# One layer on eight cores: transposes a step later, one-hot products on VectorE, and a later norm

## The reference, cut to what matters

```python
xn = layernorm(x)
q, k, v = split_heads(xn @ w_qkv.T + b_qkv)          # 16 heads of 64
q = silu(q);  k = softmax(k, over the tokens)
out = q @ (k.T @ v)                                  # linear attention, kv is 64 x 64 per head
out = layernorm(out, ln_g, ln_b)
gate = sigmoid((xn @ w_g1.T + b_g1) @ w_g2.T + b_g2) # 1024 -> 64 -> 1024
attn = (out * gate) @ w_out.T + b_out
# mixture of experts: 8 experts, top 2 per token, 769 slots per expert for 2048 tokens
top_vals, top_idx = top_k(xn @ Wr.T, 2);  w = softmax(top_vals)
pos = position of each (token, choice) in its expert # cumsum of the one-hot choices
expert_in[expert, pos] = xn[token]                   # dropped where pos >= capacity
ffn[token] = sum_k w[token, k] * (expert_in @ We)[expert_k, pos_k]
y = x + attn + ffn
```

## Time and profile before

| what | before |
|---|---|
| median of 3 runs | 545.15 us (543.25 to 560.69) |
| the profiled execution: its own time | 543.36 us |
| its span (slowest core, core 1) | 541.8 us |
| spans of the 8 cores | 532.8 to 541.8 us |
| mean granted TensorE clock, core 1 | 0.969 |
| PE busy | 463.1 us (85%) |
| DVE / ACT / POOL busy | 289.1 (53%) / 225.0 (42%) / 203.5 us (38%) |

### The profile page before, as it was taken

How to read it: one execution, slowest core, us unless ns; L and a number is a source line. 1 busy time by engine, 2 the same in 40 slices (tenths; PEclk the granted TensorE clock), 3 DMA queues, 4 the chain that set the end, 5 groups by cost and what they waited for, 6 DMA issues and landing times.

```text
span 541.8 us, 9152 instructions; the slowest of 8 cores (532.8 to 541.8 us)
## 1 busy us (share of the span) xinstructions
PE 463.1 (85%) x3072; PEld 237.3 (44%) x3072; DVE 289.1 (53%) x621; ACT 225.0 (42%) x353; POOL 203.5 (38%) x169
## 2 busy tenths in 40 slices
PE   0778999989979897997977877899999879986996
PEld 0345655544545443543424433444544434432442
DVE  5666552057776661646654664422122424639996
ACT  3497765365455531564535644433433424200000
POOL 2254346000000139331023363345446633349753
PEclk9999999999999999999988999899999979996998
DMA  8898976999407999899898269377379997356995
GB/s 204 262 290 261 203 189 132 140 169 165 78 2 256 344 164 149 97 118 146 97 134 152 67 138 295 85 200 247 117 217 253 232 313 260 141 183 233 318 315 219
DMA packets 38131, 102.73 MB, mean 190 GB/s; under 512 B 4544, under 2 KB 4672, under 8 KB 37888
## 3 DMA queue, kind: packets, MB, share of 16 engines
q0 software_dynamic: 15520, 44.34, 45.0%
q1 hardware_dynamic: 18880, 47.21, 28.2%
q10 hardware_dynamic: 3680, 10.52, 5.4%
HBM read 93.97 MB, written 37.75 MB: 243 GB/s over the span
## 4 chain that ended last, share of the span: by engine, by line
PE 65%; issue 9%; DVE 8%; DMA 6%; ACT 5%; POOL 2%; SPq 2%; DVEq 1%; another core or an unknown queue 0%; ACTq 0%; PEldq 0%; POOLq 0%
PE PS L315 58%; PE PS L319 7%; DMA wlate<-x_tm 3%; ACT stage L323 2%; SPq L79 2%; POOL stage L696 2%; DMA wlate<-wv_t 1%; DVE bst L891 1%; DMA vq<-eo_d 1%; DVE nm L754 1%; ACT vq L323 1%; DMA eo_d<-vq,dtab 1%; ACT stage L330 1%; DVE stage L339 1%; POOL wr L334 1%
## 5 line engine op out<-in xcount | busy, mean ns | idle before, releaser
L315 PE MATMUL PS<-wr,xnt 128*128 128x512 bf16 x512 | 119.6, 391 | 13.7 <-DVE wr L334 7.0
L315 PE MATMUL PS<-xnt,wr 128*128 128x512 bf16 x512 | 119.6, 380 | 0.5 <-ACT vq L323 0.5
L315 PEld LDWEIGHTS PS<-wr,xnt 128*128 128x128 bf16 x512 | 49.8, 100 | 76.0 <-issue 23.1
L315 PE MATMUL PS<-wlate,stage 128*128 128x512 bf16 x288 | 70.9, 398 | 5.0 <-issue 4.8
L315 PEld LDWEIGHTS PS<-xnt,wr 128*128 128x128 bf16 x512 | 47.8, 98 | 51.5 <-issue 3.5
L330 ACT COPY stage<-PS 128x1024 bf16<-128x1024 bf16 x56 | 56.4, 1008 | 16.4 <-PE PS L319 16.2
L334 POOL TENSOR_TENSOR stage<-stage 128x1024 bf16<-128x1024 f32 x16 | 34.2, 2138 | 45.5 <-DVE stage L331 39.8
L315 PE MATMUL PS<-wr,stage 128*128 128x512 bf16 x224 | 50.6, 379 | 0.2 <-issue 0.2
L338 DVE TENSOR_SCALAR vq<-PS,wslot_f 128x512 bf16<-128x512 f32 x24 | 18.0, 750 | 58.6 <-PE PS L315 45.6
L315 PEld LDWEIGHTS PS<-wlate,stage 128*128 128x128 bf16 x288 | 28.0, 101 | 35.9 <-issue 10.2
L994 POOL DMA_INDIRECT eo_d<-vq,dtab x24 | 25.0, 1041 | 48.3 <-ACT vq L323 32.7
(11 more groups left out here) (153 smaller groups left out, 645.4 us busy)
## 6 DMA issues: line engine op xcount, KB each, us to landing
wlate<-x_tm SPq DMA_DIRECT2D x20, 512.0 KB, 6.2
eo_d<-stage SPq DMA_DIRECT2D x4, 2048.0 KB, 15.3
vq<-eo_d SPq DMA_DIRECT2D x16, 512.0 KB, 5.9
xn_d<-stage SPq DMA_DIRECT2D x16, 256.0 KB, 6.6
wlate<-we POOLq DMA_DIRECT2D x2, 2048.0 KB, 34.2
wr<-we POOLq DMA_DIRECT2D x2, 2048.0 KB, 31.1
wb_d<-we POOLq DMA_DIRECT2D x8, 512.0 KB, 18.9
wlate<-wb_d SPq DMA_DIRECT2D x8, 512.0 KB
```

Source lines behind the costliest of these rows:

```text
L315: return PE.run(lambda e: e.matmul(out, l, r, start=start, stop=stop), *toks, sig=sig)
```

## The change

Five edits:

1. **K**: the transposes run three steps behind the projection and K times V four steps behind, with a fourth `eT` buffer. The loop has one more step.
2. The first two Q projections are issued in the steps at the end of the K loop; their Silus stay where they were.
3. The five one-hot products move from POOL to DVE, each a route piece of its own. At b = 0 the units 0 to 4 take the four spreads and the first product; at b = 1 unit 0 takes two products, units 1 and 2 one each. `r_table` stays at b = 1, u = 4.
4. `g_hidden` takes its bank in turn with the Q projections (banks 0 and 1), not bank 6.
5. `a_norm` is cut in two: `a_shift` (the small DVE step) stays at odd u; the activation is queued at the next even u, behind that unit's Tanh. `m_trans(0)` uses bank 1.

```diff
-        eT = [ek[:, 512 * i:512 * (i + 1)] for i in range(3)]
+        eT = [ek[:, 512 * i:512 * (i + 1)] for i in (0, 1, 2, 5)]
...
-            SPREAD = 5
+            SPREAD = 4 + NV
...
-            def r_hot():
-                for v in range(NV):
-                    tk["hot"] = GP.run(lambda e, v=v: e.tensor_tensor(
-                        hot_v[:, :, v, :], hot_c, wide(vals[:, v, :], NJE), ALU.mult),
-                        tk["hc"], tk["vals"])
-            piece(r_hot)
+            def r_hot(v):
+                def f():
+                    tk["hot"] = tt(DV, hot_v[:, :, v, :], hot_c, wide(vals[:, v, :], NJE),
+                                   ALU.mult, tk["hc"], tk["vals"])
+                return f
+            for v in range(NV):
+                piece(r_hot(v))
...
-                ex_tok[j] = act(eT[j % 3][:], bank[bk], AF.Exp, nb_tok[j], kv_tr.get(j - 3),
+                ex_tok[j] = act(eT[j % 4][:], bank[bk], AF.Exp, nb_tok[j], kv_tr.get(j - 4),
...
+            q_turn = itertools.cycle((0, 1))
+            def q_mm(b, oc):
+                bk = q_at[b, oc] = q_bank()          # next(q_turn)
+                for c in range(HC):
+                    p = mm(bank[bk], wv3[2][:, c, 128 * oc:128 * (oc + 1)],
+                           xnT[:, c, 512 * b:512 * (b + 1)], c == 0, c == HC - 1,
+                           t_wq, btok[bk], sig=(c == HC - 1))
+                return p
-            for j in range(NJ + 3):
-                if 2 <= j < NJ + 2:
-                    k_trans(j - 2)
+            for j in range(NJ + 4):
+                if 3 <= j < NJ + 3:
+                    k_trans(j - 3)
                 if j < NJ:
                     k_proj(j)
-                if j >= 3:
-                    k_kv(j - 3)
+                if NJ < j < NJ + 3:
+                    q_ahead[j - NJ - 1] = q_mm(0, j - NJ - 1)
+                if j >= 4:
+                    k_kv(j - 4)
                 if j < NJ:
                     k_exp(j)
...
             def q_proj(b, oc):
-                bk = oc % 2
...
+                p = q_ahead[oc] if b == 0 and oc in q_ahead else q_mm(b, oc)
+                bk = q_at[b, oc]
...
             def g_hidden(b):
-                bk = 6
+                bk = q_bank()
...
+            def a_shift(t):
+                s = t % 2
+                nm_tok[t] = ts(DV, nmr[:, s:s + 1], mv[:, s, 0:1], rs[:, s:s + 1], ALU.mult,
+                               -1.0, ALU.mult, ag2[t], n_tok.get(t - 2))
             def a_norm(t):
                 s = t % 2
-                n = ts(DV, nmr[:, s:s + 1], mv[:, s, 0:1], rs[:, s:s + 1], ALU.mult,
-                       -1.0, ALU.mult, ag2[t])
                 k = 1 + a_pair(t)
-                n_tok[t] = act(n_sb[t % 8], PS[:, 1024 * k:1024 * (k + 1)], AF.Identity, n,
+                n_tok[t] = act(n_sb[t % 8], PS[:, 1024 * k:1024 * (k + 1)], AF.Identity, nm_tok[t],
...
-                xtr[J], xgt_tok[J] = m_turn(0 if J <= BESIDE else J % 2, AC, ...
+                xtr[J], xgt_tok[J] = m_turn(1 if J == 0 else 0 if J <= BESIDE else J % 2, AC, ...
...
-                    if route and u < SPREAD:
+                    for _ in range({(1, 0): 2, (1, 1): 1, (1, 2): 1}.get((b, u), b == 0 and u < 5)):
                         route.pop(0)()
...
+                    t = 4 * (b - 1) + u // 2
                     if z >= 0:
                         a_gate(z // 8, z % 8)
+                    if u % 2 == 0 and 0 < t <= NT:
+                        a_norm(t - 1)
+                    if z >= 0:
                         a_z(z // 8, z % 8)
                     if b >= NB:
                         m_beside(b - NB, u)
-                    if 1 <= b <= NB:
+                    if 0 <= t < NT:
                         if u % 2 == 0:
-                            a_out(4 * (b - 1) + u // 2)
+                            a_out(t)
                         else:
-                            a_norm(4 * (b - 1) + u // 2)
+                            a_shift(t)
```

More of the change, by code:

```diff
@@ L1 @@
 import contextlib
+import itertools
 import numpy as np
@@ L767, in k_trans @@
                 for i in range(4):
-                    p = tr(bankh[bk][:, 128 * i:128 * (i + 1)], eT[j % 3][:, 128 * i:128 * (i + 1)],
+                    p = tr(bankh[bk][:, 128 * i:128 * (i + 1)], eT[j % 4][:, 128 * i:128 * (i + 1)],
                            ex_tok[j], btok[bk], sig=(i == 3))
@@ L822, in k_final, with q_bank @@
                 k_sum.extend([least, weights, most, last])
-            for j in range(NJ + 3):
-                if 2 <= j < NJ + 2:
-                    k_trans(j - 2)
+            q_ahead = {}
+            q_at = {}
+            q_turn = itertools.cycle((0, 1))
+            def q_bank():
+                return next(q_turn)
+            def q_mm(b, oc):
[8 more added lines that the diff above has]
+                    k_trans(j - 3)
                 if j < NJ:
                     k_proj(j)
-                if j >= 3:
-                    k_kv(j - 3)
+                if NJ < j < NJ + 3:
+                    q_ahead[j - NJ - 1] = q_mm(0, j - NJ - 1)
+                if j >= 4:
+                    k_kv(j - 4)
                 if j < NJ:
@@ L853, in build_nc @@
             n_tok = {}
+            nm_tok = {}
             ntr = {}
@@ L988, in m_trans @@
             def m_trans(J):
-                xtr[J], xgt_tok[J] = m_turn(0 if J <= BESIDE else J % 2, AC, xg[xg_at(J)], xgT[J % 3], xg_tok[J],
+                xtr[J], xgt_tok[J] = m_turn(1 if J == 0 else 0 if J <= BESIDE else J % 2, AC, xg[xg_at(J)], xgT[J % 3], xg_tok[J],
                                             mo_pe.get(J - 3))
```

## The result

The changed kernel takes 525.75 us (median, 521.93 to 528.42), the kernel before, on the same chip, 547.31: a ratio of 0.965, interval 0.958 to 0.971. It is faster, inside the range 513 to 532, 4.75 us above the forecast of 521. Some executions of every kernel run a few per cent slower on the cores of one die (cores 0 to 3 or 4 to 7) or of both; the medians include them, the ratios don't. The profiled execution took 527.23 us; its slowest core is now core 3, where before it was core 1.

A forecast was written before the change was run, and what follows sets the result against it. PE was taken to set the time, with its waits for other engines' queues to be won. 6.0 + 1.9 + 15.1 + 2.5 - 1.5 = 24.0 us off 543.36 gave 519.4, as a median 521 us, range 513 to 532.

The forecast's parts named there:

- K, -6.0: K loop: transposes three behind remove all but 0.3 of PE's 6.3 us of waits for the exponential.
- tail and table, -1.9: K's end to slot table: one 3.7 us PE hole before the third Q projection (+0.8), included in the table's 1.9 gain.
- Products: One-hot products before the slot table: 2.0 us each on DVE against 3184 ns on POOL, so the table starts earlier.
- Norm and gate, -15.1: Blocks 2 to 4: of 15.8 us of PE waits, all but 0.35 and 0.3 go.
- clock, -2.5: PE's half-speed stretches after waits: 2.5 of 3.3 us come back, bounds 0 and 5.
- the circle: Attention blocks: norm, tanh, product and statistics wait on each other, 6.51 us norm to norm against 5.19 of PE work.
- DMA, +1.5: Gather of J = 3 lands behind expert weights on POOL's queue, so PE waits 1.5 us, bounds 0 and 6.2.
- the DMA rival: Gathers for J = 3 land no earlier than before, PE waits 6.2 instead of 1.5 us: 526 us; chance 16%.
- my own signs of being wrong: Norm to norm over 6 us, the wait for J = 3 above 5 us, or a longer experts' stage.
- The norm's move doing nothing (537): Attention: waits come back in another place, only K and the table gain, 7.9 us: 537 us; chance 11%.
- POOL's price for the products: Slot table: five products on DVE take 3.2 instead of 2.0 us, table 5.9 us later: 527 us; chance 8%.
- the slower case: Attention: late DVE shifts hold ACT, so DVE waits twice per tile, 8.8 us against 6.5: 565 us; chance 5%.

The follow-up runs named there:

- u_norm: The changed kernel with the norm issued at the odd half steps again, ahead of the next gate tanh: 528.88 us, ratio 0.973.
- c_best: The changed kernel with K's last minimum and exp early, a one-column Silu, Q's third and fourth groups in free banks, table two half steps later: 521.09 us, ratio 0.958.
- after_again: The changed kernel run once more, unedited, on the same chip: 524.47 us, ratio 0.968.
- c_all: The changed kernel with K's last minimum and exp early, one-column Silu, Q's third group in bank 2, one product earlier, table later, expert 4's weights behind gathers: 522.94 us.
- n_tail: The changed kernel with K's last minimum and small exponential issued right behind the last block's exponential: 525.52 us.

## Why the prediction was right, point by point

**K, -6.0; tail and table, -1.9.** K became 5.6 to 8.5 us shorter, 7.4 in the mean, for 7.9 predicted. The waits for `ek` fell to 0.5 us. The hole was 3.00 us for 3.7, the product 2.02 us for 2.0, the table's wait 1.64 for 1.2. On the three cores at full clock K is 8.5 us shorter. Core 3, the slowest, lost some 3 us of that behind the hole, where the 40 matmuls took 11.68 us and not 8.79: the lower clock, which I had allowed for under another term.

**Products.** Right for the DVE price, and the root of tile 0 was held by the product: 2.22 us instead of 0.55, DVE waiting 0.54 for it. By the rule of the Trainium skill (SBUF — State Buffer, "Who interferes with whom") that the prediction weighed, the table was to come 0.8 us later; the trace agrees in kind, and shows 0.54 of the 0.8 as a wait.

**Norm and gate, -15.1; clock, -2.5.** The mechanism held, the first term was too large, and the clock gave back time in blocks 1 to 3 and took some behind them. PE's waits in blocks 1 to 3 fell from 11.4 us (core 1 before, 214.5 to 289.1 us) to 2.0 (core 3 after, 209 to 271 us; the line for the table left out of both).

```profile
PE PS L315 <- ACT stage L323: 7.6, 5, 2.6
PE PS L319 <- ACT stage L330: 2.4, 1, 2.4
PE PS L319 <- DVE stage L339: 1.0, 3, 0.3
PE PS L315 <- issue: 0.4, 1, 0.4
```

```profile
PE PS L316 <- ACT vq L324: 1.3, 1, 1.3
PE PS L320 <- issue: 0.4, 1, 0.4
PE PS L320 <- ACT vq L324: 0.3, 1, 0.3
```

In the experts' stage the 3.1 us wait that every core had is down to 1.3 or less on six cores and to 1.9 on cores 0 and 3; u_norm, where it returns on all eight, pins it on the norm. So the circle gave 9.4 us in these blocks and at most 3.1 behind them, 2.6 or more under the 15.1; 1.3 of what is left is one wait at expert 0's first group, where I had left 0.35. The rest of the 12.8 us that the slowest core won in blocks 1 to 3 is 3.4 us of PE's own time, which is the clock, over the 2.5 I gave. But behind expert 0's first wait of 1.3 us the lower level (1.2 GHz, granted clock 0.5) came back on six of eight cores, where the group of eight took 3.22 to 3.54 us instead of 1.89. I had read the circle as one mechanism with two symptoms; the table above bears that out, and shows that the gate's edit, beside the norm's, is worth 0.9 us.

**DMA, +1.5.** The wait came where described, 0 on five cores and 0.74, 3.79 and 5.32 us on three, within the bound of 6.2. On six cores the last weights ahead of it landed at 279.1 to 285.0 us, about as I had it (279). On cores 6 and 7 they landed at 292.1 and 289.9, later than before (289.4 and 286.4): there the queue gained nothing, as the DMA rival said. In c_best, where PE comes 4 us earlier, the wait was larger again, 7.77.

**What no term held.** "After attention all stages start earlier and keep their length" is the sentence that failed. The slowest core's experts took 187.4 us, 5.4 more than before, with the late updates: PE's 6.6 us wait and two more of 2.8 and 2.6 at branches, and the lower clock behind them. The kernel before had late updates too, 4.1 us at most. That they grew because of the change isn't shown; after_again has 6.4. Step by step for the slowest cores: 24.0 us were predicted and 16.1 came, K was 2.3 short (its clock, 101.0 to 103.9), blocks 1 to 3 were 4.8 short of norm, gate and clock together, the experts' stage grew 3.9 more than the 1.5 allowed, although a wait of 3.1 in it had shrunk, and 0.2 went in the start; the output's 3.3 came unforeseen. Without that 3.3, in part a matter of which core is the slowest, the time would lie near 529: that it came within 5 us of the forecast is partly luck. Two of my own signs of being wrong came, though the time did not: the wait for J = 3 passed 5 us on core 7, and the experts' stage got longer on the slowest core. In the mean of the cores that stage stayed (176.4 and 176.0).

**Rivals.** The norm's move doing nothing (537) is refuted by the 2 x 2 table, with 11.9 us. POOL's price for the products fell with 2.02 us, the slower case with the 5.19 us turn. The DMA rival (526) has the right number by another cause: its wait reached 3.79 and 5.32 us on cores 6 and 7, and neither was the slowest.

## What to carry to other kernels

When two edits sit in one circle of waits, undo each alone and both together: undone alone these measured 6.9 and 0.9 us, undone together 12.8, made alone 11.9 and 5.9, and any single figure would mislead. A bank whose release stands in a busy engine's queue is a term of its own: with the gate's layer in Q's banks, whatever stood ahead of its bias on DVE became a wait of PE: 2.61 us when a product was moved there (c_all), 1.77 us when PE itself came earlier (c_best). And once PE is fed, part of what is won early goes to whatever is paced by DMA (up to 5.32 us here, 7.77 in c_best); cut the trace into stages on all cores and compare dies before crediting a total.

## What the runs showed of the hardware

In this case semaphore updates of PE arrived late, by up to 10.4 us, on the cores of one die at a time, in all 13 profiles with indirect gathers and scatters, and only between the first of these and the last (220 to 460 us); in the one execution with direct transfers in their place there was none. Updates of DVE, ACT and POOL were never seen late. On the same die some update records are missing, in the changed kernel 14 to 28 of DVE's and 7 to 18 of ACT's per core, so a missing record is no proof of a late update. In the profile such a delay shows as "remote" or "another core or an unknown queue". The experts' stage of that die took 3 to 9 us more than the other's; that the late updates are the whole of this isn't shown.

A table load waited for what the activation behind it waits for: 1.58 us in n_tail. In c_all and c_best, where a one-column Silu without that wait went ahead, it stood directly behind the copy.
